# First mixing of an attention and FFN kernel: 32 by 32 blocks on quarters of TensorE in place of block-diagonal 128 by 128 weights

## The reference

```python
x = x + attention(condition(x, L0_cond_weights, tok))     # tok: one of 16 conditions for each batch entry
x = x + fp8_ffn(condition(x, L0_cond2_weights, tok))

def condition(x, weights, tok):        # x: (32, 32, 512), weights: (16, 32, 32)
    W = weights[tok]                   # (32, 32, 32), one block for each batch entry
    return jnp.einsum('bct,bcd->bdt', x, W)
```

## Time and profile before

| | |
|---|---|
| time, median of 3 runs (lowest to highest) | 518.03 us (517.9 to 518.78) |
| the profiled execution, its time | 518.72 us |
| its span, first to last instruction | 516.8 us |
| mean granted clock of TensorE | 0.997 |
| TensorE busy with matmuls | 504.7 us, 98% of the span |
| VectorE, ScalarE, GpSimd busy | 413.0, 251.4, 310.4 us |
| share of TensorE in the chain that ended last | 87% |

### The profile page before, as it was taken

How to read it: one execution, slowest core, us unless ns; L and a number is a source line. 1 busy time by engine, 2 the same in 40 slices (tenths; PEclk the granted TensorE clock), 3 DMA queues, 4 the chain that set the end, 5 groups by cost and what they waited for, 6 DMA issues and landing times.

```text
span 516.8 us, 9293 instructions
## 1 busy us (share of the span) xinstructions
PE 504.7 (98%) x3184; PEld 406.0 (79%) x3184; DVE 413.0 (80%) x648; ACT 251.4 (49%) x481; POOL 310.4 (60%) x308
## 2 busy tenths in 40 slices
PE   8999999999999999999999999999999999999994
PEld 6888888877888888888888888888888888778634
DVE  5459867899698969896888789877978788985696
ACT  2552644564446444644464537354735453423364
POOL 1658688988659756975697569747884653400000
PEclk9999999999999999999999999999999999999998
DMA  8345121320502050204020502050310006000004
GB/s 263 125 156 186 46 82 63 101 69 15 164 1 61 3 163 0 61 0 162 0 61 0 162 0 61 0 162 4 114 46 20 2 1 208 2 2 1 0 0 164
DMA packets 32645, 35.29 MB, mean 68 GB/s; under 512 B 2251, under 2 KB 22859, under 8 KB 32620
## 3 DMA queue, kind: packets, MB, share of 16 engines
q1 hardware_dynamic: 32620, 34.96, 21.0%
HBM read 28.66 MB, written 6.29 MB: 68 GB/s over the span
## 4 chain that ended last, share of the span: by engine, by line
PE 87%; DVE 6%; POOL 3%; issue 2%; DMA 1%; ACT 0%; SPq 0%; DVEq 0%; POOLq 0%; ACTq 0%
PE bank L743 23%; PE bank L744 22%; PE bank L745 22%; PE bank L813 3%; PE bank L802 3%; PE bank L715 3%; PE bank L717 3%; PE bank L716 3%; PE bank L686 1%; POOL q_rot L401 1%; PE bank L871 1%; POOL wq_lo L387 1%; PE bank L697 1%; DVE y L1319 1%; DVE xacc L1339 1%
## 5 line engine op out<-in xcount | busy, mean ns | idle before, releaser
L401 POOL TENSOR_TENSOR q_rot<-q_rot,q_swap 128x512 f32<-128x512 f32 x64 | 88.2, 1379 | 60.8 <-DVE q_swap L1096 60.8
L530 ACT ACTIVATE q_swap<-bank 64x512 f32<-64x512 f32 x80 | 47.7, 596 | 124.3 <-PE bank L745 76.9
L743 PE MATMUL bank<-wo_hi,o_hi 128*128 128x512 f32 x256 | 101.3, 396 | 0.8 <-issue 0.6
L744 PE MATMUL bank<-wo_lo,o_hi 128*128 128x512 f32 x256 | 99.8, 390 | 0.0
L745 PE MATMUL bank<-wo_hi,o_lo 128*128 128x512 f32 x256 | 99.7, 390 | 0.0
L1144 DVE TENSOR_TENSOR xacc<-xacc,bank 128x512 f32<-128x512 f32 x64 | 43.6, 681 | 37.1 <-PE bank L745 37.1
L1096 DVE TENSOR_TENSOR q_swap<-q_swap,cst 128x512 f32<-128x512 f32 x80 | 60.2, 753 | 0.0
L743 PEld LDWEIGHTS bank<-wo_hi,o_hi 128*128 128x128 f32 x256 | 48.0, 188 | 13.1 <-issue 2.6
L745 PEld LDWEIGHTS bank<-wo_hi,o_lo 128*128 128x128 f32 x256 | 48.1, 188 | 10.2
L744 PEld LDWEIGHTS bank<-wo_lo,o_hi 128*128 128x128 f32 x256 | 48.1, 188 | 9.5
L396 POOL TENSOR_TENSOR wo_lo<-raw_o,wo_hi 128x512 fp32r<-128x512 f32 x32 | 45.5, 1445 | 9.5 <-ACT wo_hi L516 9.5
(11 more groups left out here) (165 smaller groups left out, 1047.6 us busy)
## 6 DMA issues: line engine op xcount, KB each, us to landing
raw_q<-in_L_attn_wq SPq DMA_DIRECT2D x16, 512.0 KB, 4.0
raw_o<-in_L_attn_wo SPq DMA_DIRECT2D x8, 1024.0 KB, 7.0
v_st<-values SPq DMA_DIRECT2D x16, 256.0 KB, 4.4
xacc<-in_x SPq DMA_DIRECT2D x4, 512.0 KB, 7.2
raw_k<-in_L_attn_wk SPq DMA_DIRECT2D x8, 256.0 KB, 4.3
out<-xacc SPq DMA_DIRECT2D x8, 256.0 KB, 2.5
values<-v_more SPq DMA_DIRECT2D x6, 256.0 KB, 2.1
raw_o<-in_L_attn_wv SPq DMA_DIRECT2D x1, 1024.0 KB, 7.8
```

Source lines behind the costliest of these rows:

```text
L401: pool.tensor_tensor(item_out(h, k), item_out(h, k), q_swap[(h + k) % 2][:], ALU.add).then_inc(rope_done, 1)
L530: act.activation(dst[0:P // 2, :], ps[P // 2:P, :], ACT.Copy)
L743: pe.matmul(dst, l_hi, r_hi, start=(i == 0), stop=False)
L744: pe.matmul(dst, l_hi, r_lo, start=False, stop=False)
```

## The change

The first mixing is done in 16 matmuls a tile in place of 4: for each chunk c and batch entry b, the 32 partitions of that entry alone are contracted, with the plain 32 by 32 block as the moving operand, and the result goes to bank b of the four-bank tensor `four_ps`. A tile takes 128 columns of each of the four banks, so that two tiles fill them. The selected blocks of the first mixing are therefore copied (`keep_first`) and no longer spread. ScalarE and VectorE read one tile's result from all four banks, in runs of 32 elements; they wait for the second tile of a pair before they drain the first, and the next pair's mixing awaits both drains of both tiles. The selection's results move to banks 6, 7, 4 and 5. The spreads for the second mixing are written in another place of VectorE's order, and `values(0)` awaits two of them, not four.

```diff
-                wbd1 = sb("wbd1", [P, TILES, BPT, T], F32, opening)
+                wmix1 = sb("wmix1", [P, TILES, T], F32, opening)
-        bank = [ctx.enter_context(nc.psum_tensor(f"bank{i}", [P, 512], F32)) for i in range(8)]
+        four_ps = ctx.enter_context(nc.psum_tensor("four_ps", [P, BPT, 512], F32))
+        bank = [four_ps[:, i, :] for i in range(BPT)] + [ctx.enter_context(nc.psum_tensor(f"bank{i}", [P, 512], F32)) for i in range(BPT, 8)]
-        h_ps = bank[0:3]
-        sel_ps = [bank[3], bank[4], bank[5], bank[7]]
+        sel_ps = [bank[6], bank[7], bank[4], bank[5]]
+        def mixed(t):
+
+            return four_ps[:, :, (t % 2) * P:(t % 2 + 1) * P].rearrange("p b (c r) -> p c b r", c=KC)
+
+        def by_block(a, t):
+            return a[:, :, t * P:(t + 1) * P].rearrange("p c (b r) -> p c b r", b=BPT)
             def h_high(t):
-                act.wait_ge(h_mm, t + 1)
-                act.activation(hT_hi[:, :, t * P:(t + 1) * P], h_ps[t % 3][:].rearrange("p (c r) -> p c r", c=KC), ACT.Copy)
+                act.wait_ge(h_mm, t + 1 if t % 2 else t + 2)
+                act.activation(by_block(hT_hi, t), mixed(t), ACT.Copy)
...
                 pe.wait_ge(wbd_done, t // 2 + 1)
                 pe.wait_ge(dma_x[t // 2], 16)
-                if t >= 3:
-                    pe.wait_ge(h_lo_done, t - 2)
+                if t % 2 == 0 and t > 0:
+                    pe.wait_ge(h_kept, t)
+                    pe.wait_ge(h_lo_done, t)
                 for c in range(KC):
-                    mm = pe.matmul(h_ps[t % 3][:, c * P:(c + 1) * P], xacc[:, t, c * P:(c + 1) * P],
-                                   wbd1[:, t, :, :], start=True, stop=True)
+                    for b in range(BPT):
+                        own = slice(T * b, T * (b + 1))
+                        first = (t % 2) * P + c * T
+                        mm = pe.matmul(four_ps[:, b, first:first + T], xacc[own, t, c * P:(c + 1) * P], wmix1[own, t, :],
+                                       start=True, stop=True)
                 mm.then_inc(h_mm, 1)
...
-                    pe.wait_ge(wbd2_done, TILES // 2)
+                    pe.wait_ge(wbd2_done, 2)
...
+            def keep_first(i):
                 dve.wait_ge(sel_mm, i + 1)
-                spread_blocks(i, 0).then_inc(wbd_done, 1)
+                dve.tensor_copy(wmix1[:, 2 * i:2 * i + 2, :], selected(i, 0)).then_inc(wbd_done, 1)
...
             def h_low(t):
-                dve.wait_ge(h_kept, t + 1)
+                dve.wait_ge(h_kept, t + 1 if t % 2 else t + 2)
```

More of the change, by code:

```diff
@@ L457, in h_high @@
             def h_high(t):
-                act.wait_ge(h_mm, t + 1)
-                act.activation(hT_hi[:, :, t * P:(t + 1) * P], h_ps[t % 3][:].rearrange("p (c r) -> p c r", c=KC), ACT.Copy)
+                act.wait_ge(h_mm, t + 1 if t % 2 else t + 2)
+                act.activation(by_block(hT_hi, t), mixed(t), ACT.Copy)
             def h_keep(t):
-                act.activation(h_full[:, :, t * P:(t + 1) * P], h_ps[t % 3][:].rearrange("p (c r) -> p c r", c=KC),
-                               ACT.Copy).then_inc(h_kept, 1)
+                act.activation(by_block(h_full, t), mixed(t), ACT.Copy).then_inc(h_kept, 1)
             def wv_high(c):
@@ L989, in select_pair, with selected, spread_second @@
                 dve.tensor_tensor(selectors[:, i], eq_b, csel_b, ALU.mult).then_inc(sel_lhs, 1)
[L991 to L996, removed]
+            def selected(i, w):
+                return sel_ps[i][:, 0:2 * 64].rearrange("p (t w d) -> p t w d", w=2, d=T)[:, :, w, :]
+            def keep_first(i):
                 dve.wait_ge(sel_mm, i + 1)
-                spread_blocks(i, 0).then_inc(wbd_done, 1)
+                dve.tensor_copy(wmix1[:, 2 * i:2 * i + 2, :], selected(i, 0)).then_inc(wbd_done, 1)
+            def spread_second(i):
+                dve.tensor_tensor(wbd2[:, 2 * i:2 * i + 2], selected(i, 1).unsqueeze(2).broadcast_to([P, 2, BPT, T]), block_b,
+                                  ALU.mult).then_inc(wbd2_done, 1)
             def h_low(t):
-                dve.wait_ge(h_kept, t + 1)
-                cols = slice(t * P, (t + 1) * P)
-                dve.tensor_tensor(hT_lo[:, :, cols], h_ps[t % 3][:].rearrange("p (c r) -> p c r", c=KC),
-                                  hT_hi[:, :, cols].bitcast(F32), ALU.subtract).then_inc(h_lo_done, 1)
+                dve.wait_ge(h_kept, t + 1 if t % 2 else t + 2)
+                dve.tensor_tensor(by_block(hT_lo, t), mixed(t), by_block(hT_hi, t).bitcast(F32), ALU.subtract).then_inc(h_lo_done, 1)
             def v_copy(i):
@@ L1030, in _ @@
             select_pair(1)
-            spread_first(0)
+            keep_first(0)
             select_pair(2)
-            spread_first(1)
+            keep_first(1)
             select_pair(3)
-            spread_first(2)
-            spread_first(3)
+            spread_second(0)
+            spread_second(1)
+            keep_first(2)
             h_low(0)
             h_low(1)
-            for i in range(TILES // 2):
-                spread_blocks(i, 1).then_inc(wbd2_done, 1)
+            keep_first(3)
+            spread_second(2)
+            spread_second(3)
             h_low(2)
```

## The result

The changed kernel takes 524.49 us (median of 4 runs, 523.49 to 525.83) against 518.12 us for the kernel before, run beside it (4 runs, 517.9 to 518.78). The ratio is 1.0124, with a 95% interval of 1.0112 to 1.0137. It is 6.4 us **slower**; the prediction was 518.1 us and no change, with a range of 517.2 to 519.4, and is wrong.

The account below looks back on a forecast made before the run. TensorE, busy 98% of the span, was taken as the bound. The opening's 0.82 us won less 0.41 for each of two later pairs gave 0.00; 518.03 plus 0.1 for thin margins made 518.1 us, range 517.2 to 519.4.

Parts of the forecast that it names:

- rival 4: Opening: the new pairs keep less of the array busy, the clock falls, 2.3 us lost, 520.4 us; chance 0.05.
- The pace of the quarters: First mixing: quarter matmul records follow each other every 0.029 us, as in `attend`, 64 records a pair.
- rival 2: First mixing: quarters overlap less, pace 0.034 us, 1.3 us more, 519.4 us; chance 0.06.
- rival 1: First mixing: 32 moved columns give a faster pace of 0.027 us, gaining 0.6 us, 517.5 us; chance 0.14.
- Rival 5: First mixing: the four pairs shrink to a quarter of their time, giving back 5.3 us, 512.7 us; chance 0.01.
- The waits ahead of pair 2 and values(0): TensorE's opening: waits of 0.26 and 0.70 us go; `values(0)` starts at 17.84 instead of 18.66, 0.82 us won.
- Rival 3: Drains of the first mixing: reading four banks costs 0.15 us more each and becomes a wait, 519.6 us; chance 0.11.
- What is late next: Behind pair 4: `t_sum(0)` comes 1.3 us late, VectorE's idle time absorbs 1.06, product 4 still doesn't wait.
- pairs 3 and 4: Mixing pairs among the values: each costs 0.41 us more on quarters, taking back the opening's 0.82 us.

Follow-up runs that it names:

- e2: Changed kernel with the first mixing's quarter matmuls moving 128 columns (block repeated four times) instead of 32; 518.92 us, ratio 1.0011.
- e3: Kernel before, mixing on the full array but moving only 32 of the 128 columns; 522.0 us, ratio 1.0072.
- e9: Changed kernel moving each block twice, 64 columns instead of 32, with drains reading the first copy; 518.64 us, ratio 1.0002.
- e4: Changed kernel without the quarters: block-diagonal matmuls on the full array, paired drains, new banks, spread order and values(0) wait kept; 517.75 us, ratio 0.9989.
- e8: e4 with v_copy(4) ahead of t_sum(0) on VectorE; 517.45 us, ratio 0.9981.
- e7: Kernel before with only the selection's new banks, the new spread order and values(0) waiting for two spreads; 516.87 us, ratio 0.9976.
- e6: Changed kernel with 128 moved columns in the second mixing pair alone, 32 in the others; 522.98 us, ratio 1.0084.
- e5: Changed kernel with 128 moved columns in the first mixing pair alone, 32 in the others; median 518.62 us, ratio 1.0019, ten runs.
- e10: e1 with one filling matmul of 512 columns behind each of the first four tiles instead of two; median 525.61 us, ratio 1.0145.
- e1: Changed kernel plus two 512-column bf16 filling matmuls on the full array behind each tile's mixing in the first two pairs; 520.91 us, ratio 1.0044.

## Why the prediction was wrong

**The step that failed** is the one that took the pace of all of TensorE's work in the opening at full clock. The fall of the clock stood there as rival 4, "the new pairs keep less of the array busy", with a chance of 0.05 and 2.3 us. Both numbers were too low. The price was taken from the length of the warm-up, 4.57 us; the clock stayed low for 13.7 us, from about 12.2 to 25.8. By the same rule half of that, 6.8 us, would be lost, and 6.3 us were (below). The chance rested on the clock having fallen only in the tail, where TensorE idled: I read the clock as following TensorE's busy time. The windows above show it low with busy at 2.00 of 2.00. And I had the right numbers in hand: the selection moves 64 columns at about the pace at which the mixing moves 128, so the moved columns do not set that pace. The weight loads probably do: in the windows above they are busy for 1.96 of 2.00 us in the selection and the first pair, and for 3.17 of 4.00 among the values; no run varied them. At the same pace, fewer moved columns mean less work in the array. I used this against a faster pace and did not ask what it does to the clock. e2, e3 and e9 show that it decides: the pace is nearly the same in all of them, and the clock falls with 32 columns and stays with 64 or 128.

The Trainium skill ("TensorE: Matmul & The Clock Gate", The HAM clock gate) says that the gate follows how busy the array has been, and its practical rule is to leave no long idle gap between bursts of matmuls. By that rule alone the clock would have stayed, for there was no gap; the trace decides that matmuls without a gap are not enough, and e2, e3 and e9 that what they move counts.

**What was right at full clock,** by e9, which is the changed kernel with the clock held:

- *The pace of the quarters, and rival 2.* 0.029 us was taken from `attend`. In the changed kernel the third pair gives (1.99 - 0.27) / 63 = 0.027, in e9 with 64 columns (2.01 - 0.27) / 63 = 0.028, in e2 with 128 columns 0.029. So rival 1's pace came true for 32 columns, worth 0.1 us a pair, and rival 2's did not: the overlap is 0.110 / 0.027 = 4-fold. Rival 5 has no ground either, a pair taking 1.9 us as before. A pair among values costs from its last neighbour's start to the next one's 31.02 - 28.79 = 2.23 us, against 2.35 forecast and 1.94 before.
- *The waits ahead of pair 2 and values(0).* They go: 17.53 us is where values(0) starts in e9, 17.84 was forecast. From the first mixing it is 7.60 us, against 7.66 forecast and 8.56 before. The forecast's adding had a slip: 12.28 + 2.07 + 1.28 is 15.63 and not 15.67, so its margin ahead of pair 2 was 0.18 us. Nothing hangs on it.
- *The drains.* Reading four banks in runs of 32 costs nothing that the trace shows: in the changed kernel ScalarE's drains take 0.59 to 0.62 us and VectorE's two take 1.29, against 0.60, 0.62 and 1.28 before. Rival 3 had no ground in its price. Its other half, that late drains become a wait, was right at a place that I had not looked at.
- *What is late next, a term that the sum lacks.* `t_sum(0)` was forecast 1.3 us late; in e9 it is 1.1 (it starts 26.26 us after the first mixing, against 25.19 before). I followed the lateness to product 4, where TensorE did not wait, and counted VectorE's idle time ahead of `v_copy(5)` and `v_copy(6)`. I passed over `v_copy(4)`, which stands right behind `t_sum(0)` in the queue with no idle time ahead of it; `values(6)` awaits it. That missed term is 0.35 us, shown by e4's bracket and by e8, which removes it.
- *The sum at full clock.* 0.0 was forecast and 36.92 - 36.81 = +0.11 us measured; e9's ratio of 1.0002 agrees. That it comes so close is partly luck: the missed 0.35 us is offset for the most part by pairs 3 and 4, which cost 2.23 - 1.94 = 0.29 us more each and not 0.41.

**Which part of the change is worth what,** from first mixing to first key in the profiled executions: the order of the spreads and the shorter wait 35.36 - 36.81 = -1.45 us (e7, which also has the selection's other banks); the drains in pairs 36.13 - 35.36 = +0.77 (e4), of which 0.34 is one copy's place (e8); the quarters at full clock, with each block moved twice, 36.92 - 36.13 = +0.79 (e9); and the fallen clock 43.21 - 36.92 = +6.29. The sum is +6.40. Each of these is the difference of two single executions, so tenths are not certain; the medians of the whole kernels, each against the kernel before that ran beside it, give -1.54, +0.99, +0.67 and +6.25 us.

What stays open: why the clock stays low for 13.7 us in the changed kernel, 10.2 us in e3 and e6 and 6.8 us in e5, and why e5 and e10 fall in some executions only. What part the selections on both sides of the first pair have in the fall, with their 64 moved columns, was not tested either. The executions differ by some tenths of a microsecond in when the opening's stages begin, but none of these runs varied that on purpose.

## What to carry to other kernels

A full queue is not a working array. Before matmuls are cut into narrower ones, compare what sets their pace with what they move: if it is not the moved columns, narrower matmuls save little or no time and can cost the clock, for the matmuls behind them too. In an opening, where small matmuls stand beside small matmuls, look at the granted clock in windows of one or two microseconds, and measure several executions, since one kernel can have two outcomes (e5, 518.2 to 518.7 and 522.0 to 522.1 us).

Where an engine's queue is in order, follow a late instruction through everything behind it and ask of each who waits for it, not only what it waits for.

## What the runs showed that I had not expected

- Moving the same block twice, 64 columns for 32, made the kernel 5.9 us faster (e9 against the changed kernel), at 0.02 to 0.04 us more for a pair.
- On the full array, 32 columns in place of 128 saved 0.09 us in the first pair (1.75 against 1.84 from start to start), nothing in a pair among the values (1.70 both), and cost 3.7 us (e3, 522.0 against 518.3).
- The clock came down while TensorE was busy without a gap, and four matmuls of filling did not reliably hold it (e10, four runs of five at 525.6 us and more), where eight did (e1, 520.9).
